# A decoder kernel: first stage pipelined over the batch elements, layer norms with their variance on all partitions

## Chip, cores and metric

The kernel runs on one core of one Trainium2 chip. The metric is device time in microseconds, the median of several executions. The engines are TensorE (PE in the profile, PEld its weight loads), VectorE (DVE), ScalarE (ACT), GpSimd (POOL) and SyncE (SP). Four batch elements (B = 4) of 512 tokens (S) with 128 channels (D) go through four layers. Activations lie transposed, channels on the 128 partitions and tokens along the free dimension, all float32.

## The reference, cut to what matters

The first sublayer is RWKV time mixing, per element:

```python
xs = x shifted by one token
xk = x*mk + xs*(1-mk); xv, xr likewise;  K = xk Wk^T;  V = xv Wv^T;  R = xr Wr^T
w = -exp(W)
p = max(pp, U+k); e1 = exp(pp-p); e2 = exp(U+k-p); y = (e1*aa + e2*v)/(e1*bb + e2)
p2 = max(pp+w, k); e1b = exp(pp+w-p2); e2b = exp(k-p2); aa, bb, pp = e1b*aa+e2b*v, e1b*bb+e2b, p2
output = (sigmoid(R) * y) Wo^T
```

Every sublayer is followed by a layer norm of the residual sum, `(x - m) / sqrt(v + eps)` over the 128 channels; some sublayers have norms of their own, with gain and shift. One of them (`centred=False`) is a root-mean-square norm, without the mean.

## The kernel before, in words

The program is a row of stages. Each is a block with one instruction stream per engine; engines meet only through semaphores inside a stage, and all of them at its end. `rwkv` (L319) is called once for each element, and makes three stages each time, twelve in all. The first mixes tokens on VectorE (L338, L340), multiplies by three weights on TensorE (L349), and has ScalarE copy k and v out of PSUM and take the sigmoid for r (L357). The second is the recurrence. VectorE runs the running maximum as a scan (L377), four arguments (L379 to L385), the product with v and two more scans (L388 to L390), and numerator and denominator (L392 to L396), then a reciprocal (L397) and two multiplications (L398, L399). `Chain` makes VectorE wait for each of these before the next. ScalarE takes the four exponentials (L405). The third stage is `dense` (L224) with one product (L251) and its copy (L261).

`normalize_all` (L603) is called 16 times. It cuts the four elements into eight pieces of 256 tokens and runs them as a software pipeline over steps s, written out by hand in one order per engine. VectorE in step s: residual sum z(s), where there is one (L649); d(s-1) = z minus mean (L656); reciprocal of the deviation of piece s-2 (L661); scaling of piece s-3 (L666). TensorE: mean of piece s, spread to all partitions by a 128x128 matrix of 1/128 (L682); variance of s-1, as two products with one output column each, which put the variances of tokens on partitions (L690); and for s-2 two products that spread the inverse deviation back to all partitions (L699).
## Time and profile before

| | us |
|---|---|
| median of 3 runs | 5445.45 |
| lowest, highest | 5443.71, 5460.72 |
| the profiled execution, device time | 5470.13 |
| its span | 5468.3 |
| TensorE busy, share of the span | 84% |
| VectorE, ScalarE, GpSimd | 56%, 52%, 36% |
| mean granted TensorE clock | 0.901 |

Busy shares are averages over very different stages; TensorE's busy time is modelled and does not mean full use of the array. The granted clock is in parts of 2.4 GHz: 1.00 is 2.4 GHz, and the other level, 0.50, is 1.2 GHz; a stretch with both has a mean between them.

### The profile page before, as it was taken

The numbers are of one execution on the slowest core, as the hardware profiler recorded it, in microseconds if no ns is written. First come the engines' busy times: TensorE is split into PE (matmuls) and PEld (weight loads), VectorE is DVE, ScalarE is ACT, GpSimd is POOL, SyncE is SP. The second block draws the span as 40 slices with busy tenths as digits, with TensorE's granted clock in tenths as the row PEclk, the third lists the DMA queues.
The fourth block names the chain that finished last, engine by engine and source line by source line (L and its number), as shares of the span: only waits on it lengthen the run. The fifth ranks groups of instructions, "written<-read, shape, count | busy, mean of one in ns | idle before, by whom it ended". The sixth has DMA issues, their size and how long they took to land. (4 is left out here: it accounts for less than half of the span.)

```text
span 5468.3 us, 100163 instructions
## 1 busy us (share of the span) xinstructions
PE 4578.9 (84%) x36268; PEld 2790.6 (51%) x36268; DVE 3078.7 (56%) x5928; ACT 2838.8 (52%) x8700; POOL 1977.2 (36%) x2122
## 2 busy tenths in 40 slices
PE   2998869897998988988979889865557988887999
PEld 1665446575564664645646646534445664223344
DVE  6453155355664755746647557539994555662433
ACT  2453224454774765747747657457772442452522
POOL 0231000033984957939849579203331320000000
PEclk6899969899998999999999999976778998896889
DMA  0000000000111111111111111100000000000000
GB/s 33 23 1 4 2 22 9 17 2 7 45 46 38 46 46 38 41 39 46 46 38 46 46 34 45 35 20 1 1 1 11 1 4 5 10 5 32 6 0 8
DMA packets 34484, 123.02 MB, mean 22 GB/s; under 512 B 8484, under 2 KB 9512, under 8 KB 32296
## 3 DMA queue, kind: packets, MB, share of 16 engines
q1 hardware_dynamic: 33960, 116.23, 7.9%
q8 instruction: 305, 5.00, 0.4%
q14 instruction: 219, 1.79, 0.1%
HBM read 37.24 MB, written 1.05 MB: 7 GB/s over the span
## 5 line engine op out<-in xcount | busy, mean ns | idle before, releaser
L640 POOL MEMSET norm_eps<- 128x1 f32 x16 | 1.6, 98 | 1680.8 <-POOLq L116 1621.8
L2095 POOL TENSOR_TENSOR local_other<-local_raw,local_sin 128x256 f32<-128x256 f32 x768 | 557.3, 726 | 60.2
L1956 PE MATMUL ps<-arena,local_xs 128*128 128x512 f32 x768 | 438.9, 656 | 111.0 <-DVE local_raw L2136 61.5
L2092 POOL TENSOR_TENSOR local_rot<-local_raw,local_cos 128x512 f32<-128x512 f32 x384 | 488.2, 1271 | 68.4 <-DVE local_raw L2136 68.3
L2098 POOL TENSOR_TENSOR local_rot<-local_rot,local_other 128x512 f32<-128x512 f32 x384 | 486.6, 1267 | 30.1
L2069 ACT ACTIVATE ps<-ps,local_negmax 128x96 f32<-128x96 f32 x1536 | 474.2, 309 | 40.5 <-DVE local_negmax L2130 40.4
L2136 DVE SCALAR_TENSOR_TENSOR local_raw<-local_inverse,ps 128x512 f32<-128x512 f32 x384 | 264.0, 688 | 275.5 <-ACT local_inverse L2063 275.5
L2126 DVE TENSOR_REDUCE local_norm<-local_squares 128x8 f32<-128x512 f32 x384 | 263.2, 685 | 133.3 <-ACT local_squares L2038 133.3
L2038 ACT ACTIVATE local_squares<-ps 128x512 f32<-128x512 f32 x384 | 229.8, 598 | 158.1 <-PE ps L1956 157.8
L2069 ACT ACTIVATION_READ_ACCUMULATOR ps<-ps,local_negmax 128x1 f32 x1536 | 309.8, 202 | 0.0
L2001 PE MATMUL ps<-const,local_probs 128*96 128x128 f32 x1536 | 235.3, 275 | 77.8 <-DVE local_probs L2154 77.8
L1985 PE MATMUL ps<-const,local_rot 128*128 128x128 f32 x1536 | 246.3, 282 | 46.0 <-POOL local_rot L2098 45.9
L1985 PEld LDWEIGHTS ps<-const,local_rot 128*128 128x128 f32 x1536 | 175.4, 142 | 187.9 <-POOL local_rot L2098 93.2
L2001 PEld LDWEIGHTS ps<-const,local_probs 128*96 128x96 f32 x1536 | 170.6, 126 | 194.5 <-DVE local_probs L2154 102.9
L2014 PE MATMUL ps<-local_pts,local_V_span 96*64 96x64 f32 x6144 | 266.1, 230 | 0.6
L2014 PEld LDWEIGHTS ps<-local_pts,local_V_span 96*64 96x64 f32 x6144 | 212.9, 139 | 70.7 <-issue 69.5
L2077 ACT COPY local_pts<-ps 96x512 f32<-96x512 f32 x384 | 221.4, 577 | 17.8 <-PE ps L2001 17.8
L1432 DVE TENSOR_REDUCE l3a_limits<-ps 128x1 f32<-128x512 f32 x256 | 164.9, 686 | 111.3 <-PE ps L1280 111.3
L2047 ACT ACTIVATE local_Q<-ps 128x512 f32<-128x512 f32 x192 | 114.6, 597 | 217.1 <-PE ps L1985 217.1
L2154 DVE TENSOR_TENSOR local_probs<-ps,local_total 128x384 f32<-128x384 f32 x384 | 214.0, 557 | 13.2
L2130 DVE TENSOR_REDUCE local_negmax<-ps 128x4 f32<-128x384 f32 x384 | 210.4, 548 | 6.2 <-PE ps L1974 6.1
L1956 PEld LDWEIGHTS ps<-arena,local_xs 128*128 128x128 f32 x768 | 119.7, 195 | 181.5 <-DVE local_raw L2136 105.3
(527 smaller groups left out, 10969.1 us busy)
## 6 DMA issues: line engine op xcount, KB each, us to landing
local_V_span<-local_V SPq DMA_DIRECT2D x96, 384.0 KB, 4.0
local_V_span<-local_V SPq DMA_DIRECT2D x96, 256.0 KB, 3.6
arena<-in_L1f_a SPq DMA_DIRECT2D x7, 2176.0 KB, 8.5
local_V_span<-local_V SPq DMA_DIRECT2D x72, 128.0 KB, 2.3
arena<-in_L3f SPq DMA_DIRECT2D x1, 3460.0 KB, 10.9
arena<-in_L1f_f SPq DMA_DIRECT2D x6, 537.5 KB, 4.0
arena<-in_L0f SPq DMA_DIRECT2D x1, 2824.5 KB, 10.0
arena<-in_L0x SPq DMA_DIRECT2D x1, 2049.5 KB, 9.1
```

Source lines behind the costliest of these rows:

```text
L1956: nc.tensor.matmul(bank("qk", n)[:, :], tokens_of(tile), w("Wqkv", QKV[i] * 512, (QKV[i] + 1) * 512), start=True, stop=True)\
L1985: mm = nc.tensor.transpose(TURN[:, c * P:(c + 1) * P], m.rot[:, n % 4, c * P:(c + 1) * P], core.ident)
L2001: mm = nc.tensor.transpose(PT[0:SPAN, u * P:(u + 1) * P], m.probs[:, g % 2, u, :], core.ident)
L2014: mm = nc.tensor.matmul(OUT[DH * h:DH * h + DH, c * SPAN_Q:(c + 1) * SPAN_Q], m.V_span[:, tile % 2, half_span, (2 * c + h) * DH:(2 * c + h ...
L2038: nc.scalar.activation(m.squares[:, n % 2, :], bank("qk", n)[:, :], ACT.Square).then_inc(squared, 1)
L2069: nc.scalar.activation(scores, scores, ACT.Exp, bias=m.negmax[:, s % 2, u:u + 1], accum_out=m.total[:, s % 2, u:u + 1])\
L2077: nc.scalar.copy(m.pts[:, g % 3, :, :].rearrange("p u q -> p (u q)"), PT[0:SPAN, :])\
L2092: link(nc.gpsimd.tensor_tensor(rot, raw, m.cos[:, t, a * DH:(a + 1) * DH].unsqueeze(1) .broadcast_to([P, 8, DH]), ALU.mult))
L2095: link(nc.gpsimd.tensor_tensor(other[:, :, lo:lo + HALF], raw[:, :, HALF - lo:DH - lo], m.sin[:, t, a * DH + lo:a * DH + lo + HALF].unsque ...
L2098: nc.gpsimd.tensor_tensor(rot, rot, other, ALU.add).then_inc(rotated, 1)
L2126: nc.vector.tensor_reduce(m.norm[:, n % 4, :], heads(m.squares[:, n % 2, :]), AX_X, ALU.add)\
L2136: nc.vector.scalar_tensor_tensor(out=heads(m.raw[:, n % 4, :]), in0=m.inverse[:, n % 4, :].unsqueeze(2).broadcast_to([P, 8, DH]), scalar=1 ...
```

## The change

`rwkv_all` replaces the twelve stages by one stage for all elements. Token mixing goes into the weights: W_now = W * mix and W_past = W - W_now are made once, and each projection is a sum of two products, with the tokens and with the shifted tokens. All engines work in a software pipeline over b with buffers in pairs. The sigmoid becomes exp(-R), plus one on GpSimd, multiplied into the denominator; the reciprocal becomes exp(-log(den)) on ScalarE. In `normalize_all` the variance product uses the whole 1/128 matrix and gives 256 columns on all partitions; the inverse deviation is exp(-0.5 * log(var + eps)) on 128x256 on ScalarE. The spreading products and the reciprocal are gone, and the pipeline is one step shorter. Both load the table set with log and exp at their start.

```diff
@@ -316,97 +316,164 @@
-def rwkv(core):
...
+def rwkv_all(core):
     nc = core.nc
     w = core.weights("L0a", None)
+    KINDS = "kvr"
+    before, now = slice(0, S), slice(1, S + 1)
+    with core.stage() as st, ExitStack() as mem:
+        def tmp(name, shape):
+            return mem.enter_context(nc.sbuf_tensor(f"rwkv_{name}_{nc.next_id()}", shape, F32))
+        W_now, W_past, decay = tmp("W_now", [P, 3, P]), tmp("W_past", [P, 3, P]), tmp("decay", [P, 2])
+        k, v, r = (tmp(n, [P, 2, S]) for n in KINDS)
+        PP, AA, BB = (tmp(n, [P, S + 1]) for n in ("PP", "AA", "BB"))
+        e1b, e2b, e1, e2, pmax, kv, own, den, log = (tmp(n, [P, S]) for n in ("e1b", "e2b", "e1", "e2", "pmax", "kv",
+                                                                              "own", "den", "log"))
+        num, inverse = tmp("num", [P, 2, S]), tmp("inverse", [P, S])
...
+        neg_decay = decay[:, 1:2]
+        def bank(kind, b):
+            return core.ps[2 * KINDS.index(kind) + b % 2]
+        def out(b):
+            return core.ps[6 + b % 2]
...
+        @st.block.gpsimd
+        def _(pool):
+            for b in range(B):
+                here = r[:, b % 2, :]
+                pool.wait_ge(read["r"], b + 1)
+                nc.gpsimd.tensor_scalar(here, here, 1e30, 1.0, ALU.min, ALU.add).then_inc(r_done, 1)
+        @st.block.tensor
+        def _(pe):
+            def project(b):
+                pe.wait_ge(weighed, b + 1)
+                if b >= 2:
+                    pe.wait_ge(stored, b - 1)
+                nc.tensor.matmul(out(b)[:, :], w("Wo"), num[:, b % 2, :], start=True, stop=True).then_inc(projected, 1)
+            for b in range(B):
+                X = core.tokens[:, b, PAD:PAD + S]
+                Xs = core.tokens[:, b, PAD - 1:PAD - 1 + S]
+                for i, kind in enumerate(KINDS):
+                    if b == 0:
+                        pe.wait_ge(split, 2 * (i + 1))
+                    if b >= 2:
+                        pe.wait_ge(read[kind], b - 1)
+                    nc.tensor.matmul(bank(kind, b)[:, :], W_now[:, i, :], X, start=True, stop=False)
+                    nc.tensor.matmul(bank(kind, b)[:, :], W_past[:, i, :], Xs, start=False, stop=True)\
+                      .then_inc(ready[kind], 1)
+                if b >= 2:
+                    project(b - 2)
+            for b in range(B - 2, B):
+                project(b)
+        @st.block.scalar
+        def _(act):
+            def take(b):
+                act.wait_ge(ready["k"], b + 1)
+                if b >= 2:
+                    act.wait_ge(args_ready, 4 * (b - 1))
+                nc.scalar.copy(k[:, b % 2, :], bank("k", b)[:, :]).then_inc(read["k"], 1)
+                act.wait_ge(ready["v"], b + 1)
+                if b >= 2:
+                    act.wait_ge(den_ready, b - 1)
+                nc.scalar.copy(v[:, b % 2, :], bank("v", b)[:, :]).then_inc(read["v"], 1)
+                act.wait_ge(ready["r"], b + 1)
+                if b >= 2:
+                    act.wait_ge(den_ready, b - 1)
+                nc.scalar.activation(r[:, b % 2, :], bank("r", b)[:, :], ACT.Exp, scale=-1.0).then_inc(read["r"], 1)
+            def store(b):
+                act.wait_ge(projected, b + 1)
+                nc.scalar.copy(core.sums[:, b, :], out(b)[:, :]).then_inc(stored, 1)
+            nc.scalar.preload_act_table_set("natural_log_exp_and_others")
+            nc.scalar.activation(decay[:, 0:1], w("W"), ACT.Exp).then_inc(decayed, 1)
+            take(0)
+            for b in range(B):
+                for i, e in enumerate((e1b, e2b, e1, e2)):
+                    act.wait_ge(args_ready, 4 * b + i + 1)
+                    nc.scalar.activation(e[:, :], e[:, :], ACT.Exp).then_inc(exp_ready, 1)
+                if b + 1 < B:
+                    take(b + 1)
+                if b >= 1:
+                    store(b - 1)
+                act.wait_ge(den_ready, b + 1)
+                nc.scalar.activation(log[:, :], den[:, :], ACT.Ln).then_inc(log_ready, 1)
+                act.wait_ge(log_ready, b + 1)
+                if b >= 1:
+                    act.wait_ge(weighed, b)
+                nc.scalar.activation(inverse[:, :], log[:, :], ACT.Exp, scale=-1.0).then_inc(inv_ready, 1)
+            store(B - 1)
+        @st.block.vector
+        def _(dve):
+            link = Chain(dve, step)
+            for i, kind in enumerate(KINDS):
+                nc.vector.tensor_scalar(W_now[:, i, :], w("W" + kind), w("mix_" + kind), None, ALU.mult).then_inc(split, 1)
+                dve.wait_ge(split, 2 * i + 1)
+                nc.vector.tensor_tensor(W_past[:, i, :], w("W" + kind), W_now[:, i, :], ALU.subtract).then_inc(split, 1)
+            dve.wait_ge(decayed, 1)
+            link(nc.vector.tensor_scalar(neg_decay, decay[:, 0:1], -1.0, None, ALU.mult))
+            link(nc.vector.memset(PP[:, 0:1], -1e38))
+            link(nc.vector.memset(AA[:, 0:1], 0.0))
+            link(nc.vector.memset(BB[:, 0:1], 0.0))
+            def finish(b):
+                dve.wait_ge(inv_ready, b + 1)
+                nc.vector.tensor_tensor(num[:, b % 2, :], num[:, b % 2, :], inverse[:, :], ALU.mult)\
+                  .then_inc(weighed, 1)
+            for b in range(B):
+                K, V, N = k[:, b % 2, :], v[:, b % 2, :], num[:, b % 2, :]
+                dve.wait_ge(read["k"], b + 1)
+                nc.vector.tensor_tensor_scan(PP[:, now], neg_decay.broadcast_to([P, S]), K, -1e38, ALU.add, ALU.max)\
+                  .then_inc(scan_done, 1)
+                dve.wait_ge(scan_done, b + 1)
                 nc.vector.scalar_tensor_tensor(out=e1b[:, :], in0=PP[:, before], scalar=neg_decay, in1=PP[:, now],
                                                op0=ALU.add, op1=ALU.subtract).then_inc(args_ready, 1)
+                nc.vector.tensor_tensor(e2b[:, :], K, PP[:, now], ALU.subtract).then_inc(args_ready, 1)
+                link(nc.vector.scalar_tensor_tensor(out=pmax[:, :], in0=K, scalar=w("U"), in1=PP[:, before],
                                                     op0=ALU.add, op1=ALU.max))
                 nc.vector.tensor_tensor(e1[:, :], PP[:, before], pmax[:, :], ALU.subtract).then_inc(args_ready, 1)
+                nc.vector.scalar_tensor_tensor(out=e2[:, :], in0=K, scalar=w("U"), in1=pmax[:, :],
                                                op0=ALU.add, op1=ALU.subtract).then_inc(args_ready, 1)
+                if b >= 1:
+                    finish(b - 1)
+                dve.wait_ge(exp_ready, 4 * b + 2)
+                dve.wait_ge(read["v"], b + 1)
+                link(nc.vector.tensor_tensor(kv[:, :], e2b[:, :], V, ALU.mult))
                 link(nc.vector.tensor_tensor_scan(AA[:, now], e1b[:, :], kv[:, :], 0.0, ALU.mult, ALU.add))
                 link(nc.vector.tensor_tensor_scan(BB[:, now], e1b[:, :], e2b[:, :], 0.0, ALU.mult, ALU.add))
+                dve.wait_ge(exp_ready, 4 * b + 4)
+                if b >= 2:
+                    dve.wait_ge(projected, b - 1)
+                if b >= 1:
+                    dve.wait_ge(log_ready, b)
+                link(nc.vector.tensor_tensor(N, e1[:, :], AA[:, before], ALU.mult))
+                link(nc.vector.tensor_tensor(own[:, :], e2[:, :], V, ALU.mult))
+                link(nc.vector.tensor_tensor(N, N, own[:, :], ALU.add))
+                link(nc.vector.tensor_tensor(own[:, :], e1[:, :], BB[:, before], ALU.mult))
+                link(nc.vector.tensor_tensor(own[:, :], own[:, :], e2[:, :], ALU.add))
+                dve.wait_ge(r_done, b + 1)
+                nc.vector.tensor_tensor(den[:, :], own[:, :], r[:, b % 2, :], ALU.mult).then_inc(den_ready, 1)
+            finish(B - 1)
@@ -610,17 +677,16 @@
     HALF = S // 2
     pieces = [(i, slice(h * HALF, (h + 1) * HALF)) for i in range(len(items)) for h in range(2)]
     N = len(pieces)
-    LAST = N + 4
+    LAST = N + 3
     with core.stage() as st, ExitStack() as mem:
         def tmp(name, shape):
             return mem.enter_context(nc.sbuf_tensor(f"norm_{name}_{nc.next_id()}", shape, F32))
-        z, d, sq, std = tmp("z", [P, 4, HALF]), tmp("d", [P, 4, HALF]), tmp("sq", [P, 2, HALF]), tmp("std", [P, 2, 2])
-        epsc, warm = tmp("eps", [P, 1]), tmp("warm", [P, 1])
...
-        mean, var, inv = core.ps[0:2], core.ps[2:4], core.ps[4:6]
+        z, d, sq = tmp("z", [P, 4, HALF]), tmp("d", [P, 4, HALF]), tmp("sq", [P, 2, HALF])
+        log, inverse, epsc = tmp("log", [P, 2, HALF]), tmp("inverse", [P, 2, HALF]), tmp("eps", [P, 1])
...
+        mean, var = core.ps[0:2], core.ps[2:4]
...
-                k = s - 2
-                if 0 <= k < N:
-                    dve.wait_ge(std_ready, k + 1)
-                    nc.vector.reciprocal(std[:, k % 2, :], std[:, k % 2, :]).then_inc(inv_ready, 1)
                 k = s - 3
                 if 0 <= k < N:
                     i, cols = pieces[k]
-                    dve.wait_ge(spread, k + 1)
+                    dve.wait_ge(inv_ready, k + 1)
                     nc.vector.scalar_tensor_tensor(out=items[i][1][:, cols], in0=centre(k),
-                                                   scalar=1.0 if gain is None else gain, in1=inv[k % 2][:, 0:HALF],
+                                                   scalar=1.0 if gain is None else gain, in1=inverse[:, k % 2, :],
                                                    op0=ALU.mult, op1=ALU.mult).then_inc(done, 1)
...
-                        pe.wait_ge(std_ready, k - 1)
-                    for t in (0, 1):
-                        mm = nc.tensor.matmul(var[k % 2][:, t:t + 1], sq[:, k % 2, t * P:(t + 1) * P],
-                                              core.average[:, 0:1], start=True, stop=True)
-                    mm.then_inc(var_ready, 1)
-                k = s - 2
-                if 0 <= k < N:
-                    pe.wait_ge(inv_ready, k + 1)
-                    if k >= 2:
-                        pe.wait_ge(done, k - 1)
-                    for t in (0, 1):
-                        mm = nc.tensor.matmul(inv[k % 2][:, t * P:(t + 1) * P],
-                                              std[:, k % 2, t:t + 1].broadcast_to([P, P]), core.ident,
-                                              start=True, stop=True)
-                    mm.then_inc(spread, 1)
+                        pe.wait_ge(log_ready, k - 1)
+                    nc.tensor.matmul(var[k % 2][:, 0:HALF], core.average, sq[:, k % 2, :], start=True, stop=True)\
+                      .then_inc(var_ready, 1)
         @st.block.scalar
         def _(act):
+            nc.scalar.preload_act_table_set("natural_log_exp_and_others")
             act.wait_ge(eps_ready, 1)
-
-            nc.scalar.activation(warm[:, :], epsc[:, :], ACT.Sqrt).then_inc(warmed, 1)
...
-                        act.wait_ge(spread, k - 1)
-                    nc.scalar.activation(std[:, k % 2, :], var[k % 2][:, 0:2], ACT.Sqrt, bias=epsc[:, 0:1])\
-                      .then_inc(std_ready, 1)
+                        act.wait_ge(inv_ready, k - 1)
+                    nc.scalar.activation(log[:, k % 2, :], var[k % 2][:, 0:HALF], ACT.Ln, bias=epsc[:, 0:1])\
+                      .then_inc(log_ready, 1)
+                    act.wait_ge(log_ready, k + 1)
+                    if k >= 2:
+                        act.wait_ge(done, k - 1)
+                    nc.scalar.activation(inverse[:, k % 2, :], log[:, k % 2, :], ACT.Exp, scale=-0.5)\
+                      .then_inc(inv_ready, 1)
...
-        for b in range(B):
-            core.work_on(b)
-            rwkv(core)
+        rwkv_all(core)
         residual_norm_all(core, core.sums)
```

## Rows read from the trace of the kernel before

**Rows 1.** The page, busy time of each engine over the whole span.
```profile
PE 4578.9 (84%) x36268; PEld 2790.6 (51%) x36268; DVE 3078.7 (56%) x5928; ACT 2838.8 (52%) x8700; POOL 1977.2 (36%) x2122
```

**Rows 2.** Windows view, the first stage: length, busy time (instructions) by engine, granted clock, DMA.
```profile
10.80:123.64 112.84, 27.94 (x32) 9.21 (x32) 75.43 (x100) 31.84 (x45) 0.00 (x0) 0.59 0.03 11
```

**Rows 3.** Timeline, first element: start, length, engine, line, operation, tiles, count, idle before.
```profile
10.80 0.69 DVE L338 TENSOR_TENSOR rwkv_diff<-tokens 128x512 f32<-128x512 f32 x1 [9.87 <-PEq L3351]
...
12.33 2.08 PE L349 MATMUL ps<-rwkv_xk,rwkv 128*128 128x512 f32 x2 [12.33 <-DVE rwkv_xk L340]
...
14.45 0.60 ACT L357 ACTIVATE rwkv_k<-ps 128x512 f32<-128x512 f32 x1 [2.19 <-PE ps L349]
...
19.34 1.23 DVE L377 TENSOR_TENSOR_SCAN rwkv_PP<-rwkv_decay,rwkv_k 128x512 f32<-128x512 f32 x1
...
23.38 1.29 ACT L405 ACTIVATE rwkv_e<-rwkv_e 128x512 f32<-128x512 f32 x2 [0.76 <-DVE rwkv_e L384]
23.92 0.68 DVE L388 TENSOR_TENSOR rwkv_kv<-rwkv_e2b,rwkv_v 128x512 f32<-128x512 f32 x1
...
27.16 0.69 DVE L392 TENSOR_TENSOR rwkv_num<-rwkv_e,rwkv_AA 128x512 f32<-128x512 f32 x1
...
30.79 3.35 DVE L397 RECIPROCAL rwkv_kv<-rwkv_kv 128x512 f32<-128x512 f32 x1
...
36.14 2.05 PE L251 MATMUL ps<-rwkv_num,rwkv 128*128 128x512 f32 x2 [18.32 <-PEq L116]
38.22 0.60 ACT L261 ACTIVATE sums<-ps 128x512 f32<-128x512 f32 x1 [13.55 <-PE ps L251]
...
39.12 0.69 DVE L338 TENSOR_TENSOR rwkv_diff<-tokens 128x512 f32<-128x512 f32 x1 [3.53 <-PEq L116]
```

**Rows 4.** Windows view, norms from the constant's write to the last result; sum over 16.
```profile
123.64:143.34 19.70, 18.32 (x80) 15.69 (x80) 10.71 (x32) 6.24 (x18) 0.10 (x1) 0.64 0.00 1
...
665.35:681.20 15.85, 13.72 (x80) 10.21 (x80) 9.93 (x32) 6.24 (x18) 0.10 (x1) 1.00 0.00 1
...
1325.08:1338.61 13.53, 12.02 (x80) 9.99 (x80) 6.98 (x24) 6.02 (x18) 0.10 (x1) 1.00 0.01 1
...
sum 272.95, PE 248.53 PEld 209.66 DVE 140.39 ACT 93.86 POOL 1.55; mean PE 15.53 PEld 13.10 DVE 8.77 ACT 5.87 POOL 0.10
```

**Rows 5.** Timeline of TensorE in the first norm at the low clock.
```profile
129.92 1.06 PE L682 MATMUL ps<-norm_z,const 128*128 128x256 f32 x2
...
130.78 0.85 PE L690 MATMUL ps<-const,norm_sq 128*128 128x1 f32 x4
...
131.49 1.20 PE L699 MATMUL ps<-const,norm_std 128*128 128x128 f32 x4
...
132.48 1.06 PE L682 MATMUL ps<-norm_z,const 128*128 128x256 f32 x2
```

**Rows 6.** Timeline of TensorE and ScalarE in the fifth norm at the full clock.
```profile
675.04 0.42 ACT L718 ACTIVATE norm_sq<-norm_d 128x256 f32<-128x256 f32 x1 [1.34 <-DVE norm_d L656]
...
676.64 0.70 PE L682 MATMUL ps<-norm_z,const 128*128 128x256 f32 x2
676.95 0.42 ACT L718 ACTIVATE norm_sq<-norm_d 128x256 f32<-128x256 f32 x1 [1.34 <-DVE norm_d L656]
677.27 0.24 ACT L724 ACTIVATE norm_std<-ps,norm_eps 128x2 f32<-128x2 f32 x1
```

**Rows 7.** Groups of ScalarE by line and shape: count, busy us, mean ns, idle before.
```profile
L2060 ACT ACTIVATE local_log<-local_norm,local_tiny 128x8 f32<-128x8 f32 x384 | 113.8, 296 | 56.6 <-DVE local_norm L2126 56.6
...
L2723 ACT ACTIVATE ssm_dA<-ssm_dt,ssm_rate 128x160 f32<-128x160 f32 x192 | 64.6, 420 | 0.0
...
L2029 ACT ACT_TABLE_LOAD x6 | 7.7, 1283 | 46.0 <-PEq L122 46.0
```

**Rows 8.** One line of VectorE: duration ns min/median/max.
```profile
L2841 DVE TENSOR_TENSOR ssm_H<-ssm_H,ssm_scratch x52: 383/391/799, 3685.2 to 4118.6; 128x128 f32<-128x128 f32 x52
```

**Rows 9.** One line of GpSimd: duration ns min/median/max.
```profile
L851 POOL TENSOR_TENSOR l1x_probs<-l1x_powers,l1x_total x64: 1038/1039/1042, 1074.5 to 1314.2; 128x512 f32<-128x512 f32 x64
```

More of the change, by code:

```diff
@@ new lines, in rwkv_all, with _ @@
+    KINDS = "kvr"
[9 more added lines that the diff above has]
+        num, inverse = tmp("num", [P, 2, S]), tmp("inverse", [P, S])
+        ready = {n: st.sem(n + "_ready") for n in KINDS}
+        read = {n: st.sem(n + "_read") for n in KINDS}
+        r_done, decayed, step, split, args_ready, exp_ready, den_ready, log_ready, inv_ready = (
+            st.sem(n) for n in ("r_done", "decayed", "step", "split", "args_ready", "exp_ready", "den_ready",
+                                "log_ready", "inv_ready"))
+        projected, stored, scan_done = st.sem("projected"), st.sem("stored"), st.sem("scan_done")
+        weighed = st.sem("weighed")
+        neg_decay = decay[:, 1:2]
[3 more added lines that the diff above has]
+            return core.ps[6 + b % 2]
+        @st.block.sync
+        def _(sp):
+            sp.sem_clear(st.stale)
+        @st.block.gpsimd
[84 more added lines that the diff above has]
+                dve.wait_ge(scan_done, b + 1)
@@ L379, in _ @@
                 nc.vector.scalar_tensor_tensor(out=e1b[:, :], in0=PP[:, before], scalar=neg_decay, in1=PP[:, now],
                                                op0=ALU.add, op1=ALU.subtract).then_inc(args_ready, 1)
-                nc.vector.tensor_tensor(e2b[:, :], k[:, :], PP[:, now], ALU.subtract).then_inc(args_ready, 1)
-                link(nc.vector.scalar_tensor_tensor(out=pmax[:, :], in0=k[:, :], scalar=w("U"), in1=PP[:, before],
+                nc.vector.tensor_tensor(e2b[:, :], K, PP[:, now], ALU.subtract).then_inc(args_ready, 1)
@@ L390, in _ @@
                 link(nc.vector.tensor_tensor_scan(BB[:, now], e1b[:, :], e2b[:, :], 0.0, ALU.mult, ALU.add))
-                dve.wait_ge(exp_ready, 4)
-                link(nc.vector.tensor_tensor(num[:, :], e1[:, :], AA[:, before], ALU.mult))
-                link(nc.vector.tensor_tensor(kv[:, :], e2[:, :], v[:, :], ALU.mult))
-                link(nc.vector.tensor_tensor(num[:, :], num[:, :], kv[:, :], ALU.add))
-                link(nc.vector.tensor_tensor(kv[:, :], e1[:, :], BB[:, before], ALU.mult))
@@ L396, in _ @@
-                link(nc.vector.tensor_tensor(kv[:, :], kv[:, :], e2[:, :], ALU.add))
-                link(nc.vector.reciprocal(kv[:, :], kv[:, :]))
-                link(nc.vector.tensor_tensor(num[:, :], num[:, :], kv[:, :], ALU.mult))
-                link(nc.vector.tensor_tensor(num[:, :], num[:, :], r[:, :], ALU.mult))
-            @st.block.scalar
-            def _(act):
-                for i, e in enumerate((e1b, e2b, e1, e2)):
-                    act.wait_ge(args_ready, i + 1)
-                    nc.scalar.activation(e[:, :], e[:, :], ACT.Exp).then_inc(exp_ready, 1)
@@ L407, in rwkv @@
-        dense(core, 1, lambda j, m: w("Wo"), lambda j: num[:, :], lambda m: core.Y[:, :])
+                dve.wait_ge(exp_ready, 4 * b + 4)
[6 more added lines that the diff above has]
+                link(nc.vector.tensor_tensor(N, N, own[:, :], ALU.add))
@@ L616, in tmp @@
             return mem.enter_context(nc.sbuf_tensor(f"norm_{name}_{nc.next_id()}", shape, F32))
-        z, d, sq, std = tmp("z", [P, 4, HALF]), tmp("d", [P, 4, HALF]), tmp("sq", [P, 2, HALF]), tmp("std", [P, 2, 2])
-        epsc, warm = tmp("eps", [P, 1]), tmp("warm", [P, 1])
-        z_ready, mean_ready, d_ready, sq_ready, var_ready, std_ready, inv_ready, spread, done, eps_ready, warmed = (
-            st.sem(n) for n in ("z_ready", "mean_ready", "d_ready", "sq_ready", "var_ready", "std_ready",
-                                "inv_ready", "spread", "done", "eps_ready", "warmed"))
-        shifted = st.sem("shifted")
-        mean, var, inv = core.ps[0:2], core.ps[2:4], core.ps[4:6]
+        z, d, sq = tmp("z", [P, 4, HALF]), tmp("d", [P, 4, HALF]), tmp("sq", [P, 2, HALF])
+        log, inverse, epsc = tmp("log", [P, 2, HALF]), tmp("inverse", [P, 2, HALF]), tmp("eps", [P, 1])
+        z_ready, mean_ready, d_ready, sq_ready, var_ready, log_ready, inv_ready, done, shifted, eps_ready = (
+            st.sem(n) for n in ("z_ready", "mean_ready", "d_ready", "sq_ready", "var_ready", "log_ready", "inv_ready",
+                                "done", "shifted", "eps_ready"))
+        mean, var = core.ps[0:2], core.ps[2:4]
         def summed(k):
```

52 lines of the change are left out of this document (removed).

## The prediction

> **What bounds the kernel now.** The page's busy shares come first [rows 1]: TensorE 84%, nothing else over 56%. This says little here, as the change touches two kinds of stage that hold 112.8 + 273 of 5468 us. So the windows view comes second. In the first stage VectorE is busy 75.4 of 112.8 us, TensorE 27.9 and ScalarE 31.8 [rows 2]: no engine is full, the three take turns. The timeline of one element shows why [rows 3]: mixing at 10.80, products at 12.33, k out of PSUM at 14.45, the first scan only at 19.34, the output product at 36.14, its copy at 38.22, and the next element's mixing at 39.12. 28.32 us an element, four in a row, nothing overlapped. In it VectorE's reciprocal takes 3.35 us.
>
> The 16 norms are the third look, again as windows [rows 4]: 272.95 us in sum, TensorE busy 248.5 of them. Six run at clock 1.00, like those of 15.85 and 13.53 us; ten lie between 0.57 and 0.81, like the first, 19.70 us at 0.64. The timeline says what sets the pace at the low level [rows 5]: TensorE goes from mean (129.92) to variance (130.78) to spreading (131.49) to the next mean (132.48) without a pause, 2.56 us a piece. At the full clock the fifth norm takes 1.91 us a piece (Squares at 675.04 and 676.95, [rows 6]), and ScalarE has waited 1.34 us before its Square.
>
> **First stage, to the first scan.** The scan of element 0 stands at 19.34 because the stage with the products must end. Now it waits only for k. Two 128x128 operations of VectorE come before the first product instead of two of 512 columns (1.53 us, from 10.80 to 12.33). A 128x128 one takes 0.39 [rows 8]; between 0 and 1.53, I take 0.7, so 11.5. The first product had its result read 2.12 us after its start [rows 3]; a second accumulates on it. A pair of 256 columns occupies TensorE for 0.86 at the low clock [rows 5], so one of 512 takes 1.72. k is ready at 15.3, copied by 15.95 (0.60 and a handover), and the scan starts there. ScalarE takes k, v and r before the exponentials, which are queued behind r: v comes 3.44 later, r again 3.44, at 22.2 if the clock stays low, at 18.8 if all is at the high one. I take 21. Exp of r 0.60, two exponentials of about 0.64 (1.29 for two, [rows 3]): the product with v starts at 22.9, not at 15.95 + 4.58 = 20.5.
>
> **One element.** From scan to that product VectorE needs 23.92 - 19.34 = 4.58; with the two later scans to 27.16, 3.24; then five chained operations in 3.63, 0.73 each [rows 3]. The denominator's product and the moved last multiplication (`finish`) are 0.66 and 0.62, as unchained ones. Sum 12.73. Reciprocal (3.35 + 0.04) and mixing are gone. ScalarE has per element four exponentials, three copies, one store, log and exp: 6 x 0.64 + 4 x 0.60 = 6.2. TensorE has seven products: 12.0 at the low clock, 6.0 at the full one. So VectorE is the bound, narrowly at the low clock. The new waits: `finish(b-1)` waits for log and exp, done 1.4 after the denominator, and is reached 4.6 after it; the scans queued behind it do not wait. ScalarE's `store(b-1)` waits for the output product, which can start 5.2 into the element and ends by 7.4; the log queued behind is due at 12.7. TensorE waits for `weighed(b-2)` with the products of b+1 queued behind: they can start near 7 of one element and are needed in the next. These I cost at nothing; without this cover each would cost the 2 to 3 us that it lasts.
>
> **GpSimd's part.** One `min, add` of 512 columns per element is hidden by time (r is read at the end), but not by place. A GpSimd multiplication of 512 columns takes 1.04 [rows 9], and VectorE's L2841, two inputs in SBUF, goes from 0.39 to 0.80 at its worst [rows 8], where GpSimd's multiplications run beside it. So VectorE may lose between nothing and 1.04 per element, and it may gain nothing from GpSimd, which took no part in the stage before. I take 0.7, 2.8 in sum. The Trainium skill (SBUF — State Buffer, "Who interferes with whom") says that a VectorE instruction with two SBUF inputs contends with a GpSimd one that reads SBUF, and that the later blocks until the other is done: this speaks against the change, and the rise of L2841 agrees. By the rule the whole GpSimd operation is lost, near 1 us each, 4 in sum; by the row's 0.41 it is 1.6.
>
> **Its end.** First denominator: 22.9 + 3.24 + 3.63 + 0.70 = 30.5. Three more elements: 38.2. GpSimd: 2.8. 71.5. Then log and exp 1.36, last multiplication 0.74, product 2.13, copy 0.60, change of stage 0.30 [rows 3]: 76.6. The norm began at 123.64. Gain 47.0, between 40 (TensorE in the way at the low clock: 14 an element) and 52.
>
> **The norms.** At the low clock TensorE now has two products of 256 columns, 2 x 0.86 = 1.72 a piece in place of 2.56. At the full clock they are 0.86 (half), and ScalarE becomes the bound: Square, 0.32 to the next start [rows 6], then log, then exp. Neither exists at this shape: Square of 256 columns takes 0.42 [rows 6]; an activation with a scale or bias read per partition takes 0.42 for only 160 columns [rows 7], so log some 0.47 and exp, which has none, 0.42. The wait of exp for log adds 0.03, exp 0.34 to the next start. 1.16 a piece, and with VectorE's three operations (1.26 with their handovers) in between I take 1.22. Filling: residual sum 0.42, mean 0.75 (0.70 for the pair, [rows 6]), d 0.47, Square 0.47, variance 0.75, log 0.50, exp 0.47, scaling 0.42: 4.25, and 1.1 more with both products at the low clock. So a norm is 4.25 + 7 x 1.22 = 12.8 at the full clock, 5.35 + 7 x 1.72 = 17.4 at the low one; where there is no residual sum, 0.4 to 1 less. Means 12.4 and 17.1. The share at the low level is 2 x (1 - clock), 0.72 for the first; over the ten it sums to 6.5 norms ([rows 4] has the first of the 16, two at the full clock and the sum). 6.5 x 17.1 + 9.5 x 12.4 = 229. Gain 273 - 229 = 44. If log and exp cost as little as Square both (0.32 each), 52; if ScalarE's handovers cost 0.2 more a piece, 25 less.
>
> The clock may come sooner: half of TensorE's time in a piece went to products of one column and their weight loads [rows 5], and now all of it goes to wide ones without a pause; in the first stage the clock was 0.59 in the mean at 25% busy [rows 2]. If the low shares fall from 6.5 to 3.5 norms, 3 x 4.7 = 14 more. I take 4 of them.
>
> **Table sets.** The load at a norm's start (1.28 [rows 7]) lies beside residual sum and mean, as now in 12 norms; four more appear under the same cover. The uncentred norm has none: it begins with Square and may lose up to 1.3, left to the range. Nothing for the cross attentions, whose own load of the exp set should go but was followed by a wait for VectorE.
>
> **Sum.** 47 + 44 + 4 = 95. The profiled execution, 5470.1, would be 5375. It lies 24.7 above the median of the runs; the two stretches are taken to be as long in both, so the median goes from 5445.5 to 5350.5.
>
> **Rivals.**
> The forecast, 0.62: 5350.5, its own range 5338 to 5366.
> *The clock follows at once*, 0.17: all 14 in the norms and r at 18.8; with 10 and 2 to 4 more, 5338 down to 5324 where the first stage's tail is at the full clock too. For it: the denser stream. Against: VectorE-bound elements leave TensorE half idle at the full clock.
> *The norms give nothing*, 0.13: ScalarE's chain takes the place of TensorE's, or TensorE stays low in norms now at 1.00 (17.1 against 13.5 to 15.9). Then 5445.5 - 47 = 5398, half of it 5376. For it: ScalarE goes from 5.9 to some 11 us busy a norm. Against: 1.22 is under 1.91, and the norm of 13.53 us had seven spacings and a filling of TensorE's three products in it.
> *The change does not do what it says: table loads between log and exp*, 0.03, the other side. Log and exp served from different sets would put two loads of 1.28 around each pair: 2 x 1.28 x (128 + 4) = 338 us, 5350.5 + 338 = 5688. It decides from 38 pairs on (38 x 2.56 = 97). Against: L2060 and its exp run 384 times with six loads [rows 7].
> *The first stage slowed by GpSimd and TensorE together*, 0.05: 14 an element and 4 for GpSimd, gain 42: 5355.5, inside the range.
>
> **From these.** A measurement of this kernel tells 0.3%, 16 us, from no change. Faster by more: 0.96 (all but the fourth case and 0.01 of the third, in which later stages would lose clock as well); within: 0.01; slower: 0.03. Range 5322 to 5378; outside it lie the far end of the third case, the fourth, and a little below the second.
>
> **What would show it.** Right: the first norm's constant near 77 us; scans about 13 apart; no table load between stage start and first norm; norms of 12 to 13 us at clock 1.00, spacing 1.72 at the low level with TensorE unbroken; VectorE operations near GpSimd's min-add stretched by up to 1. Wrong: scans over 14 apart waiting for k; the 16 norms summing to over 245; table loads above 60 in all; later stages at a lower clock than before.

## The result and the profile after

The changed kernel takes 5387.36 us (median of 4 runs, 5385.87 to 5402.3), the kernel before 5444.84 on the same chip: ratio 0.9885, interval 0.9856 to 0.9915. The forecast was 5350.5, its range 5322 to 5378. The time went down by 57.5 us where 95 were expected.

First the page: busy time of each engine over the span. Against [rows 1] TensorE falls by 43 us, and neither it nor the others tell where the missing time is.

```profile
span 5384.8 us, 98536 instructions
PE 4535.6 (84%) x35524; PEld 2696.3 (50%) x35524; DVE 3041.0 (56%) x5774; ACT 2904.6 (54%) x8810; POOL 1985.9 (37%) x2126
```

Then the windows view of the changed stages: length, busy time (instructions) by engine, granted clock, share of DMA, GB/s. In order: the first stage (before: 112.84, [rows 2]), the first norm, the fifth (with a residual sum), one without, and the sum over all 16 (before: 19.70, 15.85, 13.53 and 272.95, [rows 4]).

```profile
10.85:72.34 61.49, 32.51 (x56) 12.43 (x56) 52.33 (x74) 24.85 (x42) 8.38 (x5) 0.73 0.05 21
72.34:86.19 13.85, 11.07 (x32) 6.30 (x32) 9.27 (x24) 10.74 (x25) 0.10 (x1) 0.84 0.01 2
590.91:603.50 12.59, 9.26 (x32) 5.13 (x32) 9.36 (x24) 10.83 (x25) 0.10 (x1) 1.00 0.00 1
1243.49:1255.04 11.55, 8.95 (x32) 5.43 (x32) 6.50 (x16) 10.37 (x25) 0.10 (x1) 1.00 0.01 1
sum 208.71, PE 163.78 PEld 97.71 DVE 124.40 ACT 171.28 POOL 1.56; mean PE 10.24 PEld 6.11 DVE 7.77 ACT 10.70 POOL 0.10
```

The first stage gains 51.3 us (123.64 to 72.34) and the norms 64.2: together 115.5, more than forecast. The two profiled spans differ by only 83.5 (5468.3 and 5384.8). The stretches between norms, compared one by one, show the rest: the last cross attention (the stage called `l3x`), which the diff doesn't touch, has grown from 218.85 to 256.59 us with the same 1224 products. All others together are 5.7 shorter (115.5 - 37.7 + 5.7 = 83.5). Its row before, then its row after; the clock is the second number from the end but two.

```profile
4987.90:5206.75 218.85, 185.47 (x1224) 83.70 (x1224) 84.68 (x189) 82.77 (x156) 4.66 (x5) 0.77 0.08 23
```

```profile
4875.99:5132.58 256.59, 225.54 (x1224) 96.58 (x1224) 86.38 (x189) 82.77 (x155) 4.66 (x4) 0.62 0.07 20
```

Cut where the clock changes, the stage after shows two long low stretches, of 58 us and of 123.6 to the stage's end. Between them the clock is full. The kernel before has the first of them too, just as long, but its second lasts 10.2 us, with the clock full for 51.2 behind it and low again for the last 24: the two rows behind those of the stage after. So what is lost lies in the second.

```profile
4899.70:4957.70 58.00, 48.91 (x254) 23.23 (x252) 19.70 (x41) 14.24 (x27) 0.00 (x0) 0.50 0.04 8
4957.70:5008.90 51.20, 46.49 (x431) 21.68 (x430) 28.20 (x65) 29.20 (x56) 0.00 (x0) 1.00 0.06 11
5008.90:5132.50 123.60, 113.50 (x487) 43.47 (x485) 32.48 (x74) 36.34 (x68) 0.00 (x0) 0.50 0.01 2
```

```profile
5012.00:5070.00 58.00, 49.27 (x257) 23.43 (x260) 19.82 (x41) 14.37 (x28) 0.00 (x0) 0.50 0.04 9
5121.20:5131.40 10.20, 9.55 (x46) 4.24 (x50) 2.67 (x5) 3.13 (x6) 0.00 (x0) 0.50 0.08 17
```

At the full clock TensorE does 8.4 products a us and is busy 91%; in the last stretch 3.9 a us, busy 92%. It isn't idle there and yet stays at 1.2 GHz. Most products of this stage are narrow in one direction, as this row of its timeline shows (weights of 32 rows and 77 columns):

```profile
5013.07 1.06 PE L1347 MATMUL ps<-l3x_Q_limited,l3x_K 32*77 32x512 f32 x1
```

### The profile page after: what moved, and what is told of

The parts are those of the page before. It is cut to its first block and busy times, and to the rows that moved or that the text cites. A ratio compares the mean times of both kernels' runs of the same rounds, so it can differ in the third digit from the quotient of the medians.

```text
span 5384.8 us, 98536 instructions
## 1 busy us (share of the span) xinstructions
PE 4535.6 (84%) x35524; PEld 2696.3 (50%) x35524; DVE 3041.0 (56%) x5774; ACT 2904.6 (54%) x8810; POOL 1985.9 (37%) x2126
## 5 line engine op out<-in xcount | busy, mean ns | idle before, releaser
L2068 PEld LDWEIGHTS ps<-local_pts,local_V_span 96*64 96x64 f32 x6144 | 213.4, 139 | 72.2 <-issue 71.0
```

The lines of the kernel that those rows point to most:

```text
L2068: mm = nc.tensor.matmul(OUT[DH * h:DH * h + DH, c * SPAN_Q:(c + 1) * SPAN_Q], m.V_span[:, tile % 2, half_span, (2 * c + h) * DH:(2 * c + h ...
```

## The experiments

Theory A: the change gains some 115 to 120 us in every run, and part of it is given back in the last cross attention, whose narrow products can leave TensorE at 1.2 GHz for long; how long depends on the moment at which the stage starts. Rivals: the new norm ahead of the stage lowers the clock by what it does; the changed first stage does; GpSimd is behind it; the stage was merely short in one profile and long in another by chance. Each was told apart by the stage's length and by "the rest" (span less that stage).

**Both kernels again** (no edit).

> The kernel before, unchanged, for a second profile. The profiled execution of before was 25 us over its median. Theory A (the granted clock makes single stretches of a stage long or short from one execution to the next): a profile near 5445 has one low-clock stretch of about 50 us fewer than the first, in a stage that the change does not touch, most likely the last cross attention (between the 14th and 15th norm, 237 us in the first profile), and the same norms and first stage within 1 us. Theory B (the 25 us are spread over all stages by profiling): every stage is a little shorter or none is.

> The changed kernel again, for a second profile. Theory A: 5386 with the low stretch of 130 us in the last cross attention, as in the first profile, or about 5350 without it. Theory B: the same profile as the first, stage by stage.

The kernel before: span 5443.0, the stage 203.56 at clock 0.83, rest 5239.4; the 16 norms 267.5. The changed one: span 5406.7, the stage 277.67 at 0.56, rest 5129.0. Their medians were 5455.37 (ratio 0.9998, 0.9976 to 1.002) and 5408.82 (0.9907, 0.9878 to 0.9937). In the second, one low stretch lasts 211.6 us:

```profile
4874.03:5151.70 277.67, 247.77 (x1224) 108.46 (x1224) 88.20 (x190) 82.89 (x156) 4.67 (x5) 0.56 0.06 18
4895.60:5107.20 211.60, 197.37 (x1000) 88.03 (x999) 72.10 (x154) 63.80 (x121) 0.00 (x0) 0.50 0.03 6
```

So the stage differs between two executions of the same kernel (256.59 and 277.67; 218.85 and 203.56). The rest hardly differs in the changed one (5128.2 and 5129.0), and by 10 us in the kernel before (5249.5 and 5239.4). Chance in each execution doesn't explain it: the two sets of runs of the changed kernel don't overlap (5385.87 to 5402.3, and 5407.45 to 5413.0). Something that holds for a whole set, the chip perhaps, takes part; no run separates it.

**Each part alone.** The kernel before with one function of the change:

```
 e2: - def normalize_all(...)   # mean, variance and spreading by one column
     + def normalize_all(...)   # that of the changed kernel
 e3: - for b ...: rwkv(...)
     + rwkv_all(core)           # that of the changed kernel, norms as before
```

> The 16 norms as after the change, the first stage as before. Theory A (the change itself gains 51 us in the first stage and 64 in the norms, and 38 us are given back in the last cross attention because the norm before it ends in another phase of the clock): norms sum near 209 us against 273; time 5444.8 - 64 = 5381 if the last cross attention keeps its clock, 5419 if it goes low as after the change. Theory B (the norms' gain is given back by the stages behind them in general): time near 5444 - 20, the loss spread over many stages.

> The first stage as after the change, the norms as before. Gain in the first stage near 51 us by both theories: 5394. If the last cross attention goes low by its phase alone, it may do so here too although nothing near it is changed: then 5394 + up to 38. If only the new norm in front of it causes it, it stays at some 219 us after the norm.

The norms alone: 5392.8 us, ratio 0.9879 (0.9832 to 0.9927), norms 210.4. The first stage alone: 5402.21, ratio 0.9891 (0.9844 to 0.9939), first norm's constant at 72.2. Each profile with its stage `l3x`, norms alone first:

```profile
4925.37:5128.52 203.15, 170.00 (x1224) 77.74 (x1224) 83.73 (x190) 82.91 (x155) 4.66 (x4) 0.83 0.08 25
```

```profile
4929.63:5141.02 211.39, 178.11 (x1224) 80.59 (x1224) 84.28 (x190) 82.77 (x156) 4.66 (x5) 0.79 0.08 24
```

With the new norm directly ahead of it the stage takes 203.15: the norm's content is not what lowers its clock. By medians on that chip (before: 5454.73) the parts gain 61.9 and 52.5, 114.4 in sum; both at once, 45.9. Of these three kernels only the one with both shows the long low stretch. Outside the stage the parts do add up: the rest is 5179.9 and 5189.8, which is 66 and 56 under the mean of the kernel before (5246, table below), 122 in sum, and both at once gain 120.

**Wide products in the stage.** Six products of 128x128 weights by 512 columns, whose result nobody reads, at steps 5 and 22 of one group:

```
+ if g == 0 and plan.name == "l3x" and s in (5, 22):
+     for _ in range(6):
+         nc.tensor.matmul(LIMIT_BANKS[(GROUPS * n) % RING][:, :], core.ident, core.const[:, 0:S], start=True, stop=True)
```

> The changed kernel with six more full 128x128x512 products on TensorE in each of two steps (5 and 22) of the last cross attention; their results are overwritten. They cost 12 x 0.86 = 10 us at the full clock. Theory A (the change gains 115 us, and the last cross attention, whose own products use 32 rows or 32 columns of the array, hangs at 1.2 GHz for 130 to 210 us while TensorE is busy without a pause; what ends a low stretch is work that fills the array): the stage between the 14th norm's end and the 15th norm falls from 257 to 278 us to 200 to 215 with the extra work in it, the time to 5335 to 5350. Theory B (the low stretch is set by something else, and wide products do not end it): the stage grows by 10 to 20 us, 5395 to 5430.

> The same twelve products in the kernel before. Theory A: 5440 to 5455, the stage at 200 to 215 as in the changed kernel, so that the two kernels now differ by 105 to 115 us and not by 46 to 58. Theory B: 5455 to 5465, and the difference stays where it was.

In the changed kernel: 5345.23 us (5343.13 to 5346.94), ratio 0.9789 (0.9768 to 0.981). In the kernel before: 5453.35, 0.9998 (0.9982 to 1.0013). More work on the engine at fault makes the changed kernel faster and leaves the other alone. The stage in the changed kernel, four of its stretches, and the first of its two bursts of wide products:

```profile
4874.06:5088.86 214.80, 181.25 (x1248) 82.32 (x1248) 83.54 (x190) 82.91 (x155) 4.66 (x4) 0.84 0.08 24
4895.80:4923.10 27.30, 18.86 (x81) 11.06 (x79) 7.59 (x16) 2.54 (x5) 0.00 (x0) 0.50 0.06 11
4923.10:4998.20 75.10, 69.13 (x623) 31.62 (x623) 39.81 (x90) 40.98 (x78) 0.00 (x0) 1.00 0.05 10
4998.20:5005.00 6.80, 6.03 (x10) 2.57 (x9) 0.75 (x1) 0.59 (x1) 0.00 (x0) 0.50 0.09 17
5005.00:5063.00 58.00, 53.82 (x434) 22.33 (x433) 25.06 (x59) 31.91 (x60) 0.00 (x0) 1.00 0.01 3
4919.42 7.12 PE L1367 MATMUL ps<-const 128*128 128x512 f32 x12
```

The low stretch that began at the same place as that of 211.6 us (4895.6 there, 4895.8 here) ends after 27.3: the burst starts at 4919.42, the clock is full from 4923.1. The second burst starts at 5001.34, the clock is full from 5005.0. But a low stretch can also end early by itself. In e1, without added work, it does after 23.9:

```profile
5000.20:5024.10 23.90, 15.84 (x84) 9.71 (x80) 7.59 (x16) 2.55 (x5) 0.00 (x0) 0.50 0.05 9
```

It is 23.9 in e6 too, where the burst had begun only 1.3 us before the clock rose, so that end isn't the burst's doing. The whole stage is 42 to 63 shorter. Both kernels now have the stage at about the same length (214.80 and 209.42), and their medians differ by 108.1: the change, with the stage's clock taken out of the comparison.

**The stage later.** Waits ahead of the stage and nothing else; 16 in e7 and e12, 6 in e11:

```
+ for i in range(16):
+     nc.vector.memset(late[:, :], 0.0).then_inc(passed, 1)
+     dve.wait_ge(passed, i + 1)
```

> The changed kernel with a stage of 16 chained VectorE memsets of 128x512 (some 6 to 9 us) ahead of the last cross attention. Theory A in its form that the moment at which the stage starts decides: another length of the low stretches in this stage, 204 to 280 us in place of 257 to 278, from the same instructions, so 5335 to 5420. A theory that the new norms themselves cause the low stretch expects the old 257 to 278 and 5395 to 5420.

> The kernel before with the same 16 memsets ahead of the last cross attention, some 8 us of waiting. By their length alone 5463. If the phase of the clock decides, this kernel too can move by more than that, either way: 5440 to 5520, the stage at 210 to 285.

> The changed kernel with a stage of 6 chained memsets (some 3 us) ahead of the last cross attention, in place of 16. If the moment of the start decides the low stretches, the stage after the norm is again another length than 230 (16 memsets) and 257 to 278 (none), anywhere from 204 to 285. If it were the wait itself that lifts the clock, less of it gives a value between those two.

e7: 5354.51 us, ratio 0.9801 (0.9779 to 0.9823). The stage takes 230.13 with some 11 us of added wait in it (the memsets last 10.4, and the block around them a little), which makes 219. e11: 5342.25, ratio 0.9802 (0.9771 to 0.9833), stage 238.81, of which some 5 are the wait. In the kernel before (e12) the same 16 cost time: 5470.06, ratio 1.0039 (1.0023 to 1.0054), stage 222.75, of which some 11 are the wait. So a wait that does no work makes the changed kernel 33 us faster than its first median and 54 faster than its second, and the kernel before 19 slower. The chip alone isn't behind it: e5, e7 and e8 (below) ran on the same one, with the stage at 214.80, 230.13 and 277.70.

The 238.81 of e11 doesn't decide as it was meant to. It lies between the lengths with 16 waits and with none, where it was expected if the wait itself lifted the clock. The traces speak against that: in e7 and e11 the low stretch behind the load of the weights is 58 us long, as in the profile after, and what is shorter is the next one, over 100 us behind the wait (10.2 and 44.4 for 129.7). Its length goes with the place in the program at which the clock falls. The table gives that place, for all profiles with a fall there, as the time from the fall to the start of the products that read `l3x_features`, to some 0.1 us:

| kernel | fall ahead of these products | low stretch |
|---|---|---|
| before, e1, e2, e7, e10 | 0.65 to 0.83 | 10.2 or 10.3 |
| e11 | 1.0 | 44.4 |
| after | 1.25 | 129.7 |
| e5, e9, wide products right behind them | 1.3, 1.25 | 6.8, 6.8 |

```profile
4999.40:5043.80 44.40, 43.63 (x226) 18.94 (x228) 15.59 (x34) 14.91 (x28) 0.00 (x0) 0.50 0.03 5
```

Half a microsecond in the place of the fall goes with 120 us of low clock. This is read from the traces; no run moved the fall alone. For the first low stretch it is less clear. The clock falls at nearly the same place in e4, e8, e12 and e5, and stays low for 211.6, 211.6 and 51.2 us, and for 27.3 in e5, the one with a burst.

**Without GpSimd.** VectorE adds the 1 itself (the clamp at 1e30 is left out), e9 with four wide products at steps 1 and 22:

```
- nc.gpsimd.tensor_scalar(here, here, 1e30, 1.0, ALU.min, ALU.add).then_inc(r_done, 1)
- dve.wait_ge(r_done, b + 1); tensor_tensor(den, own, r, ALU.mult)
+ dve.wait_ge(read["r"], b + 1)
+ scalar_tensor_tensor(out=den, in0=r, scalar=1.0, in1=own, op0=ALU.add, op1=ALU.mult)
```

> The changed kernel with GpSimd out of the first stage: the plus one goes into VectorE's denominator operation, and the clamp of exp(-R) at 1e30 is left out. The trace of the changed kernel has VectorE's BB scan at 1.45 us in place of 1.23 in two elements and 0.36 + 0.29 + 0.02 us more in the first: the stage should be 1.1 us shorter, 60.4 in place of 61.5 from 10.85 to the norm. The rule that a GpSimd operation blocks VectorE for its whole length (2.0 to 2.4 us each) would give 6 to 8. The time itself goes with the last cross attention, 5335 to 5410.

> The changed kernel without GpSimd in the first stage (the clamp of exp(-R) at 1e30 left out) and with four full products in steps 1 and 22 of the last cross attention, 8 x 0.86 = 7 us at the full clock in place of 10. If wide work early in the stage ends the low stretch (34 us after the norm's start in nearly every run), the stage is at 205 to 215 and the time 5333 to 5345, under the 5345 of the version with twelve products. If four products are too few, the stage is at 230 to 285 and the time 5360 to 5415.

e8: 5411.33, ratio 0.9915 (0.9892 to 0.9938), stage 277.70, as in e4: GpSimd is not behind the clock. From the first scan to the first norm's constant the seven profiles with GpSimd take 56.25 to 56.35 us, e8 55.16 and e9 55.35, so GpSimd costs the first stage 0.9 to 1.2 us. e9: 5351.3, ratio 0.9825 (0.9793 to 0.9857), stage 220.35, between the two outcomes that were expected (205 to 215, and 230 to 285). Its stretches and its two bursts:

```profile
4900.40:4951.60 51.20, 47.83 (x252) 23.24 (x252) 18.54 (x38) 14.24 (x27) 0.00 (x0) 0.50 0.04 7
4951.60:5002.80 51.20, 46.49 (x431) 21.66 (x430) 28.20 (x65) 29.20 (x56) 0.00 (x0) 1.00 0.05 10
5002.80:5009.60 6.80, 6.03 (x10) 2.57 (x9) 0.75 (x1) 0.58 (x1) 0.00 (x0) 0.50 0.09 17
5009.60:5067.60 58.00, 53.83 (x442) 21.93 (x441) 25.08 (x59) 32.93 (x62) 0.00 (x0) 1.00 0.02 4
4890.19 3.70 PE L1361 MATMUL ps<-const 128*128 128x512 f32 x8
5005.89 5.45 PE L1361 MATMUL ps<-const 128*128 128x512 f32 x8
```

This is the closest pair of the study. The full stretch in the middle is that of the profile after to the hundredth (51.20 us, 46.49 busy, 431 products). Then the clock falls at the same place in both; with four wide products it is back after 6.8 us, without them after 129.7 (5008.9 to 5138.6, in the next norm). The burst starts at 5005.89, the clock is full from 5009.6. The four at step 1 ran from 4890.19 to 4893.89, when the clock was still full. The low stretch that began at 4900.4 therefore says nothing on whether wide products end one; it shows that a burst ahead of a fall didn't prevent it.

So three bursts began well inside a low stretch (two in e5, one in e9), and the clock rose while each ran. A fall at the same place as in the last two, without a burst, was followed by 129.7 us of low clock (after). Not tested is whether it is the width that does it: no run put narrow products or a wait at these steps.

**More work for ScalarE in the norms.** One more Square of 256 columns in each piece:

```
+ nc.scalar.activation(spare[:, :], core.const[:, 0:HALF], ACT.Square).then_inc(spared, 1)
```

> The changed kernel with one more Square of 256 columns on ScalarE for each piece of the 16 norms, its result unused. If ScalarE sets the pace of the new norms at the full clock, as the spacing of 1.11 us says, each piece grows by 0.32 and a norm of 11.6 us by 2.2 to 2.6 us; the sum of the 16 goes from 208 to 240 to 250. If TensorE or VectorE sets it, the norms at the full clock stay within 1 us of 11.6 and 12.6 and the sum under 220.

The norms sum to 232.0 (208.71 after; 240 to 250 would have been the full price at every place):

```profile
sum 232.00, PE 163.25 PEld 100.09 DVE 124.87 ACT 205.54 POOL 1.55; mean PE 10.20 PEld 6.26 DVE 7.80 ACT 12.85 POOL 0.10
```

Norms without a residual sum at the full clock go from 11.6 to 13.5, the others from 12.6 to 14.0, those at the low clock by about 1.3. Eight Squares at 0.32 to the next start are 2.6: ScalarE is the bound at the full clock without a residual sum for three quarters of it, elsewhere it has some slack. The whole took 5363.75 us (ratio 0.9844, two runs): 34 us more busy time on ScalarE, and a faster kernel than the changed one, as its stage `l3x` came out at 203.52.

**All profiles in one table** (us; rest is span less the stage, which holds the added wait in e7, e11 and e12):

| kernel | stage `l3x` | clock | rest |
|---|---|---|---|
| before, e1, e6 (wide), e12 (late) | 218.9, 203.6, 209.4, 222.8 | 0.77, 0.83, 0.86, 0.78 | 5249.5, 5239.4, 5243.5, 5251.9 |
| after, e4 | 256.6, 277.7 | 0.62, 0.56 | 5128.2, 5129.0 |
| e5 (wide), e7, e11 (late) | 214.8, 230.1, 238.8 | 0.84, 0.75, 0.70 | 5127.4, 5132.3, 5114.5 |
| e8, e9 (no GpSimd) | 277.7, 220.4 | 0.56, 0.79 | 5126.4, 5123.1 |
| e2 (norms alone), e3 (first stage alone) | 203.2, 211.4 | 0.83, 0.79 | 5179.9, 5189.8 |
| e10 (more for ScalarE) | 203.5 | 0.83 | 5156.8 |

The means of the rest are 5246 for the four of the kernel before and 5126 for the five of the changed one with GpSimd. The change is worth 120 us outside the stage.

## Why the prediction was wrong

**The step that failed** is the sum 47 + 44 + 4 = 95. It has terms for the two changed parts alone: every other stage is put at nothing, and the 24.7 us by which the profiled execution lay over the median are carried over unchanged. The changed parts gained more than their terms (115.5). The last cross attention, put at nothing, took it back: 37.7 us longer in the two profiled executions, 53 to 74 longer than in the repeat of the kernel before (203.56). That repeat (e1, 5444.75 us) lies at the median of the kernel before, as the profile after (5386.55) does at its own. Between these two the first stage gains 51.5, the norms 58.8, the last cross attention loses 53.0, and everything else gains 1.0: 58.2 us, for the 57.5 of the medians. That later stages may lose clock stood among the signs of failure and as 0.01 of a case, where it had to be a rival with a price. The price could have been read: the stage was in the trace of before at clock 0.77 with narrow products at 1.2 GHz, and full and low clock differ there by a factor of two in products per us. The same row explains the 24.7 us by which the profiled execution lay over the median, which was carried over as a constant: against e1, 15.3 of 25.3 are this stage (218.85 and 203.56) and 5.5 the norms. After the change the excess was gone (5386.55 in the profiled run, 5387.36 median).

**First stage: 51.3 for 47, inside 40 to 52.** The mechanism held. VectorE's scans, the first copy and the end, from the timeline (start, length, engine, line, operation):

```profile
15.37 0.58 ACT L392 COPY rwkv_k<-ps 128x512 f32<-128x512 f32 x1 [3.03 <-PE ps L379]
16.07 1.23 DVE L446 TENSOR_TENSOR_SCAN rwkv_PP<-rwkv_decay,rwkv_k 128x512 f32<-128x512 f32 x1 [3.08 <-ACT rwkv_k L392]
18.81 0.60 ACT L400 ACTIVATE rwkv_r<-ps 128x512 f32<-128x512 f32 x1 [1.13 <-PE ps L379]
21.01 0.68 DVE L461 TENSOR_TENSOR rwkv_kv<-rwkv_e2b,rwkv_v 128x512 f32<-128x512 f32 x1
28.77 1.22 DVE L446 TENSOR_TENSOR_SCAN rwkv_PP<-rwkv_decay,rwkv_k 128x512 f32<-128x512 f32 x1
41.65 1.22 DVE L446 TENSOR_TENSOR_SCAN rwkv_PP<-rwkv_decay,rwkv_k 128x512 f32<-128x512 f32 x1
71.49 0.58 ACT L404 COPY sums<-ps 128x512 f32<-128x512 f32 x1 [2.89 <-PE ps L368]
```

The first scan was put at 15.95 and stands at 16.07. r is taken at 18.81, the end given for all at the high clock, not at 21, and so the product with v comes 1.9 earlier than 22.9. Scans are 12.88 apart with GpSimd's effect in it; 12.73 and 0.7 had been put. The norm's constant stands at 72.34, not near 77.

**GpSimd: 1.1 us for 2.8.** Its operation takes about twice the 1.04 of [rows 9], and VectorE hardly notices; duration ns min/median/max, then one of them beside a scan, which takes 1.45 instead of 1.23:

```profile
L360 POOL TENSOR_SCALAR rwkv_r<-rwkv_r x4: 1973/2022/2360, 19.5 to 48.5; 128x512 f32<-128x512 f32 x4
35.63 1.97 POOL L360 TENSOR_SCALAR rwkv_r<-rwkv_r 128x512 f32<-128x512 f32 x1 [8.92 <-ACT rwkv_r L400]
35.93 1.45 DVE L463 TENSOR_TENSOR_SCAN rwkv_BB<-rwkv_e1b,rwkv_e2b 128x512 f32<-128x512 f32 x1
```

By such rows VectorE loses 0.65 us in the first element (0.36 and 0.29) and 0.22 in two others, 1.1 in sum, and e8 and e9 measure 0.9 to 1.2. The Trainium skill (SBUF — State Buffer, "Who interferes with whom") has the later of two such instructions wait until the other is done. By an estimate from the lengths of these four, that would be 8 us if VectorE's were the later each time. The measurement disagrees and decides: for this pair the contention is a fraction of the overlap. VectorE's product at 21.01 takes its usual 0.68 inside a GpSimd operation that the trace has from 19.49 to 21.85.

**Norms: 64.2 for 44, and 4 for the clock.** Right: spacing 1.72 at the low clock, and TensorE unbroken:

```profile
90.76 1.06 PE L744 MATMUL ps<-tokens,const 128*128 128x256 f32 x2
91.61 1.06 PE L751 MATMUL ps<-norm_sq,const 128*128 128x256 f32 x2
92.46 1.06 PE L744 MATMUL ps<-tokens,const 128*128 128x256 f32 x2
```

At the full clock ScalarE is the chain, as put, a little faster than 1.22 (1250.25 to the next Square at 1251.36 is 1.11):

```profile
1250.25 0.40 ACT L767 ACTIVATE norm_sq<-norm_d 128x256 f32<-128x256 f32 x1
1250.55 0.45 ACT L773 ACTIVATE norm_log<-ps,norm_eps 128x256 f32<-128x256 f32 x1
1251.04 0.42 ACT L778 ACTIVATE norm_inverse<-norm_log 128x256 f32<-128x256 f32 x1
```

The mis-sized term is the share at the low clock, put at 6.5 norms, measured at 4.2. At the 4.7 us between the two levels that is 10.8. The seven norms at clock 1.00 have a mean of 12.2 (put: 12.4); 11.8 of them leave 15.4 each for the 4.2 at the low clock (put: 17.1), another 2.4 and 7 us: together the 20 between 229 and 208.7. With the denser stream of wide products the clock came sooner; the prediction saw this and took 4 of it.

**The rivals.** *The clock follows at once*: r is taken at 18.8, as it says, and the norms gain more than its 58, though their share at the low clock fell to 4.2 and not to 3.5. By its parts it was the better forecast; its time, 5324 to 5338, fails by the same step. *The norms give nothing* has a time nearer to the measured one (5398), for a reason that e2 refutes. *Table loads between log and exp*: one load per norm, none between log and exp, 54 in all, and those at the cross attentions are gone. *GpSimd and TensorE slow the first stage*: no, 12.88.

**What stays open.** Why a fall some tenths of a microsecond earlier should be followed by so much longer a low stretch wasn't settled, nor what places the fall, nor why the changed kernel's two sets of runs differ by 21 us. The waits of e7, e11 and e12 and the parts of e2 and e3 only show that the same products take 203 to 278 us, and that the changed kernel's two plain profiles fell at 257 and 278. Other stages vary as well, if less: e11's rest is 12 us below the others, all of it in the local transformer.

## What to carry to other kernels

Price a change against every stage whose TensorE clock isn't 1.00 in the trace, the untouched ones behind it too: a shift of their start can move tens of us either way. When two parts together gain less than the sum of each alone, compare the kernels stage by stage before blaming either part. Where a stage with narrow products hangs at the low clock, a few wide ones in the low stretch can end it: the changed kernel with them (5345.23 us, ratio 0.9789) beats both kernels. They are no gain in themselves (0.9998 in the kernel before), and have to fall into the stretch. A delay with no work in it (e11, 5342.25) comes out level but rests on luck with the moment.

## What the runs showed of the hardware

Busy is not enough for the clock. Here is a stretch of the profile after, in the last cross attention, with TensorE busy for all of its 20 us at 1.2 GHz:

```profile
5016.00:5036.00 20.00, 20.00 (x111) 8.88 (x108) 7.50 (x16) 7.40 (x14) 0.00 (x0) 0.50 0.03 6
```

The Trainium skill (TensorE: Matmul & The Clock Gate, Part 1) has activity release the throttle and names idling as what brings it back. This row doesn't agree: of its 111 products 99 use 32 rows or 32 columns, the engine had no pause, and it stayed at 1.2 GHz. The longest low stretch, 211.6 us in e4, was 93% busy. Bursts of wide products (128x128 by 512) came with its end (27.3 in e5, 6.8 in e5 and e9). That the narrowness is what holds the clock low is a reading that fits all this, not one that a run tested. In the full stretches of the same stage the same kinds of product held the clock up for 51.2 us, so narrow products keep either level rather than force the low one. Also, GpSimd's `min, add` of 512 columns took 1.97 to 2.36 us, about twice its multiplication of [rows 9]; VectorE was at work beside all four, so whether this is the operation's own length or the cost of sharing isn't shown.
